# Second-stage weights of one channel block stored in the order of the PSUM bank

## What is computed

```
x + conv(groupnorm(x, 32 groups))

def conv(x):
    bias = x @ bias_w.T + bias_b
    xf = rfftn(x.reshape(B, H, W, 4, 96), axes=(1, 2), norm='ortho')
    xr, xi = xf.real, xf.imag
    r1 = relu(xr @ w1[0] - xi @ w1[1] + b1[0])      # per block, 96 x 96
    i1 = relu(xr @ w1[1] + xi @ w1[0] + b1[1])
    r2 = r1 @ w2[0] - i1 @ w2[1] + b2[0]
    i2 = r2 @ w2[1] + i1 @ w2[0] + b2[1]
    out = irfftn(complex(r2, i2), norm='ortho')
    return out + bias
```

## Time and profile before

| | |
|---|---|
| median of 3 runs | 505.67 us (505.21 to 507.49) |
| profiled execution, its own time | 505.68 us |
| its span, first to last instruction | 503.9 us |
| granted TensorE clock, mean over the span | 0.973 |
| PE matmul busy | 467.5 us, 93% of the span |
| PE weight load busy | 406.5 us, 81% |
| DVE, ACT busy | 327.7 us (65%), 238.1 us (47%) |
| POOL busy | 15.5 us (3%) |

### The profile page before, as it was taken

How to read it: one execution, slowest core, us unless ns; L and a number is a source line. 1 busy time by engine, 2 the same in 40 slices (tenths; PEclk the granted TensorE clock), 3 DMA queues, 4 the chain that set the end, 5 groups by cost and what they waited for, 6 DMA issues and landing times.

```text
span 503.9 us, 16543 instructions
## 1 busy us (share of the span) xinstructions
PE 467.5 (93%) x6728; PEld 406.5 (81%) x6728; DVE 327.7 (65%) x769; ACT 238.1 (47%) x567; POOL 15.5 (3%) x16
## 2 busy tenths in 40 slices
PE   5476899999999999799999999969999999999997
PEld 5374788899888998599988898768987999887885
DVE  3686975678466875448756784637846687568624
ACT  3733474168333764047632683316833476325510
POOL 0031600000000000000000000000000000000000
PEclk9688999999999999989999999979999999999999
DMA  7640000340016000330004200060000600030003
GB/s 216 177 132 2 1 1 24 124 140 1 4 34 251 2 3 24 131 134 3 3 22 151 113 1 3 34 252 3 1 3 34 251 3 3 22 137 3 1 3 126
DMA packets 11636, 32.41 MB, mean 64 GB/s; under 512 B 4196, under 2 KB 5904, under 8 KB 11568
## 3 DMA queue, kind: packets, MB, share of 16 engines
q1 hardware_dynamic: 11568, 31.36, 17.8%
HBM read 15.63 MB, written 12.58 MB: 56 GB/s over the span
## 4 chain that ended last, share of the span: by engine, by line
PE 85%; DVE 6%; issue 4%; ACT 3%; DMA 1%; POOL 0%; DVEq 0%; SPq 0%; POOLq 0%; ACTq 0%
PE bank L522 85%; DVE r L992 1%; DVE o_sb L1007 1%; DVE rsum L985 1%; DMA x_sb<-in_x 1%; ACT y L815 1%; ACT junk L803 1%; DVE z L917 0%; ACT rho L850 0%; DVE extreme L1127 0%; ACT r L825 0%; DVE biasw L917 0%; ACT junk L806 0%; ACT g L820 0%; DVE rho L917 0%
## 5 line engine op out<-in xcount | busy, mean ns | idle before, releaser
L522 PE MATMUL bank<-w2s,rho 96*64 96x96 f16 (+1 forms) x3072 | 119.8, 247 | 0.0
L522 PEld LDWEIGHTS bank<-w2s,rho 96*64 96x64 f16 (+1 forms) x3072 | 107.9, 125 | 11.4 <-issue 11.2
L522 PE MATMUL bank<-biasw,y 128*128 128x384 f16 x576 | 105.4, 330 | 0.1
L522 PEld LDWEIGHTS bank<-biasw,y 128*128 128x128 f16 x576 | 78.6, 146 | 14.1 <-issue 0.2
L820 ACT ACTIVATE g<-bank 128x384 f16<-128x384 f32 x64 | 31.1, 485 | 98.3 <-PE bank L522 98.3
L522 PE MATMUL bank<-w1R,y 128*128 128x192 f16 (+3 forms) x768 | 62.0, 232 | 11.8 <-issue 7.4
L999 DVE SCALAR_TENSOR_TENSOR g<-g,bank 128x384 f16<-128x384 f16 x64 | 35.4, 553 | 55.0 <-ACT g L820 54.8
L835 ACT ACTIVATE z<-bank 128x384 f16<-128x384 f32 x72 | 35.3, 490 | 67.8 <-PE bank L522 67.8
L917 DVE SCALAR_TENSOR_TENSOR z<-bank,z 128x384 f16<-128x384 f32 x72 | 39.7, 557 | 38.0 <-ACT z L835 36.2
L522 PEld LDWEIGHTS bank<-tab,x_sb 128*128 128x128 f32 x384 | 51.2, 201 | 9.3 <-issue 6.1
L522 PE MATMUL bank<-tab,x_sb 128*128 128x128 f32 x384 | 52.8, 285 | 6.2 <-DMA x_sb<-in_x 6.0
(11 more groups left out here) (103 smaller groups left out, 423.3 us busy)
## 6 DMA issues: line engine op xcount, KB each, us to landing
x_sb<-in_x SPq DMA_DIRECT2D x16, 768.0 KB, 6.8
out<-o_sb SPq DMA_DIRECT2D x14, 768.0 KB, 3.8
y<-y SPq DMA_DIRECT2D x24, 128.0 KB, 2.8
out<-o_sb SPq DMA_DIRECT2D x8, 192.0 KB, 1.9
tab<-in_tab SPq DMA_DIRECT2D x1, 642.0 KB, 4.6
o_sb<-in_bias_wt SPq DMA_DIRECT2D x4, 144.0 KB, 2.7
b1s<-in_b1h SPq DMA_DIRECT2D x1, 384.0 KB, 5.2
o_sb<-in_w SPq DMA_DIRECT2D x2, 144.0 KB
```

The lines of the kernel that those rows point to most:

```text
L522: return nc.tensor.matmul(o, lhsT, rhs, start=start, stop=stop, **kw)
```

## The change

The columns of block 3 in `w2s` are kept in the order of the bank's words. Column `32 q + i` now holds what column `3 i + q` held, so the matmuls of block 3 write the words 3, 7, 11, ... one after the other, with one constant step of 4 words (16 bytes). The order of the sums and the results in the bank are the same. For this POOL's cast and POOL's difference are each split in two, one for blocks 0 to 2 and one for block 3, whose output is written in the permuted order; `w2_ready` counts to 2.

```diff
             if blk < 3:
                 return bank[:, 128 * blk:128 * blk + 128].rearrange("p (i q) -> p i q", q=4)[:, :, 0:3]
-            return bank[:, 3:CH:4].rearrange("p (q i) -> p i q", q=3)
+            return bank[:, 3:CH:4]
...
-        w2_parts = ([w2s[0:BC + 3, s, :, :, :].rearrange("k b a n -> k (b a n)") for s in range(2)],
-                    w2f[0:BC + 3].rearrange("k b a n -> k (b a n)"), w2scale[0:BC + 3, :])
+
+        w2_parts = [([w2s[0:BC + 3, s, 0:3, :, :].rearrange("k b a n -> k (b a n)") for s in range(2)],
+                     w2f[0:BC + 3, 0:3].rearrange("k b a n -> k (b a n)")),
+                    ([w2s[0:BC + 3, s, 3, :, :].rearrange("k a (q i) -> k a i q", q=3) for s in range(2)],
+                     w2f[0:BC + 3, 3].rearrange("k a (i q) -> k a i q", q=3))]
...
-                    pe.wait_ge(w2_ready, 1)
+                    pe.wait_ge(w2_ready, 2)
...
-            (high, rest), src, scale = w2_parts
-            do(nc.gpsimd.tensor_scalar(src, src, scale, None, ALU.mult))
-            do(nc.gpsimd.tensor_copy(high, src))
-            nc.gpsimd.tensor_tensor(rest, src, high, ALU.subtract).then_inc(w2_ready, 1)
+            whole = w2f[0:BC + 3].rearrange("k b a n -> k (b a n)")
+            do(nc.gpsimd.tensor_scalar(whole, whole, w2scale[0:BC + 3, :], None, ALU.mult))
+            for (high, _), src in w2_parts:
+                do(nc.gpsimd.tensor_copy(high, src))
+            for (high, rest), src in w2_parts:
+                nc.gpsimd.tensor_tensor(rest, src, high, ALU.subtract).then_inc(w2_ready, 1)
```

## The result

The changed kernel takes 508.42 us (median of 10 runs, 507.63 to 510.01), the kernel before 505.73 (median of 10, 505.21 to 507.58). The ratio is 1.0049 with a 95% interval of 1.0034 to 1.0064: slower by 1.7 to 3.2 us. The profiled execution took 509.08 us, its span is 507.3.

A forecast was written before the change was run, and what follows sets the result against it. The prediction took PE, busy for 93% of the span, to bound the kernel. It summed 505.68 us, 0 for block 3's matmuls and 0.8 for POOL's longer work to 506.5 us, range 489.0 to 508.5.

The forecast's parts named there:

- Block 3's matmuls: PE, 8 images x 102 matmuls of block 3: pace stays at 83.3 ns, gain 0 us.
- two periods for each aligned couple: PE's PSUM writes: two clock periods per aligned couple of words visited, plus about 8; block 3 stays at 192 + 8.
- A: Block 3's writes: only far jumps cost, so a pair takes 56.7 ns; total 495.0 us; chance 0.12.
- B: Block 3's writes: a constant step costs nothing, 43 ns per matmul; total 489.2 us; chance 0.12.
- The wait for `w2_ready`: PE before the product with w2: POOL ends at 58.73, PE comes at 69.33, so 10.6 us of cover.
- POOL's longer work: POOL's split cast and difference hold r_low and delay the first image: +0.8 us, from possible -0.4 to +3.2.
- My upper end: POOL's permuted pieces of 384 elements: at most 2.17 us each, the strided scaling's time, making +3.2 us.
- About one for one: First image: what POOL takes longer, the image takes longer, since r_low on DVE is held and DVE paces PE.
- rival C: POOL's permuted pieces run at its slow rate, 2.17 us each, holding r_low throughout; total 508.9 us; chance 0.12.
- the signs that I had named myself: Wrong if block 3's steps shrink at all, or POOL ends after 61.2 and first w2s matmul starts over 2.5 us late.
- the case that I held most likely: Whole kernel: matmuls gain nothing, POOL's work adds 0.8 us, 506.5 us in total; chance 0.64.
- Within 0.5% of before: Whole kernel: the time stays within 0.5% (2.5 us), taken as no measurable change; chance of same 0.64.

The follow-up runs named there:

- a whole new layout: Kernel before with the whole bank planar, columns laid out by the host and x's order restored by add_x's read: 471.23 us, ratio 0.9315.
- the split without permutation: Kernel before with POOL's cast and difference each split into pieces of 1152 and 384 elements, nothing permuted: 505.85 us, ratio 0.9991.
- wait filled: Changed kernel with the nine c2_bias matmuls of gi = 0 done twice in the first image: 506.89 us, ratio 1.0012 to the kernel before.
- loops exchanged: Changed kernel with POOL's permuted pieces written in order and read with a step of three elements: 505.24 us, ratio 0.9991 to the kernel before.
- double cast: Kernel before with POOL's cast of the w2 weights issued twice, without any permutation: 507.79 us, ratio 1.0038.
- POOL's new work alone: Changed kernel with block 3's old write order, POOL's split and permuted pieces kept: 508.86 us, ratio 1.0048 to the kernel before.

## Why the prediction was right, and where it wasn't

**Block 3's matmuls** were forecast at 83.3 ns and no gain; they run at 82.5. The rule from which this came, two periods for each aligned couple, was inferred from four patterns and then held for four more and for a whole new layout (470 us forecast, 471.2 measured). Its fixed part is 6 for most patterns, 8 for runs of three and for the old order of block 3; the difference is the 0.3 us that I had at nothing. Rivals A and B are refuted by the 0.165 us in the changed profile. The Trainium skill's line in "PSUM — Partial Sum Buffer", Specifications, on lines of 8 bytes agrees with the runs; its "any non-contiguous AP slows matmuls significantly" (AP is the access pattern) is too wide, since runs of 16 or 32 words and aligned couples with gaps cost nothing extra here. The Trainium skill's formula in "TensorE: Matmul & The Clock Gate", Back-to-back issue gap, which that section gives for an isolated matmul (42.5 ns for 96 columns), is met where all couples are full, 85 ns for the two of a triple, and not in the other patterns of `c2_rho`.

**The wait for `w2_ready`** never bound, as forecast: POOL ends 9.65 us before PE comes.

**POOL's longer work** is the step that was mis-sized: +0.8 us forecast, +2.46 measured. Four things were wrong in it. The permuted pieces take 2.39 and 2.23 us. My upper end for them was 2.17 each, and I argued even that away by DVE's work beside the strided scaling. The split alone, which I had at 0.2 us of POOL, took 1.19 (the split without permutation). "About one for one" was too much: 3.41 us of POOL moved the last `r_low` by 1.02, as the two extra breaks let two more `r_low` through. And the clock was missing: nothing in my sum had PE's longer wait cost it 1.44 us afterwards, although the kernel before shows it at the loop's boundary, where PE's wait of 3.4 us ends at 213.45 and the granted clock is 0.52 from 214.3 to 217.5. The last two errors partly cancel, which is why rival C's arithmetic (one for one at the slow rate, 508.9 us) comes near the 508.4 measured with a mechanism that is only half right.

By the signs that I had named myself this part of the forecast was wrong, if narrowly, and rival C's condition was met. POOL should have ended near 59.5 us, at 61.2 at the latest; it ended at 62.95. The first `w2s` matmul was to come at most 2.5 us after 69.33; it came 3.27 later, or 2.46, just under the mark, without the later start of the scaling. POOL's phase is 3.41 us longer, and C was to decide from 2.5 on. Block 3's steps also shrank, though by 1% only.

So the total, 508.42, is inside the range of 489.0 to 508.5 with 0.08 us to spare. It is there partly by luck, since the case that I held most likely, 506.5 us, had the main cost a third of its size. "Within 0.5% of before" is met or missed by a hair: 0.53% between the medians, a ratio of 1.0049 with an interval of 0.34 to 0.64%.

## What to carry to other kernels

Read a matmul's cost from the distance of starts for each output pattern, and write PSUM in runs that fill aligned couples of f32 words; permute the columns of the moving operand in the host's layout, and let the engine that reads the bank undo it. If POOL has to permute, try both orders of the loops: here the one with a long run written was the cheaper. Where one engine's setup holds another, put the waits that follow on the bill: a TensorE wait of 2.3 us cost 1.4 us more after it had ended, and useless matmuls in it gave those back.

## What was unexpected of the hardware

Filling a wait of PE with nine superfluous matmuls took 1.4 us off. An exchange of the two inner loops of a POOL cast of 384 elements (written in groups of 3 elements 64 bytes apart, or in one run) changed it from 2.39 to 1.18 us. `r_low`, which reads and writes SBUF, was held by every POOL instruction, up to 3.5 us for an instruction of 0.56, while `rsum`, which reads PSUM, kept its 0.54 us beside the same POOL instructions. Why the one is held and the other isn't was not tried. PE's waits for `r` of 0.68 (before), 0.89 (wait filled) and 0.95 us (loops exchanged) were followed by a granted clock of 1.00, and those of 1.79 (double cast), 2.32 and 2.33 us (the change, POOL's new work alone) by one of 0.50 to 0.52.
